# Centring three experts' first-layer weights on chip instead of their products, in a perceiver layer with KAN experts

## The chip, the cores and the metric
One core of one Trainium2 chip runs the whole kernel. The metric is the device time of one execution in microseconds; lower is better. The matrix engine is TensorE (PE in the profile), the elementwise engines are VectorE (DVE), ScalarE (ACT) and GpSimd (POOL), and SyncE (SP) starts transfers. Each has its own in-order queue of instructions; they wait for each other with semaphores.

## What is computed
A block of three parts over x (4 x 128 tokens, 128 features): cross attention on 2048 keys, a small attention over the four batch entries, and a mixture of experts. Only the last part is touched:

```python
logits = x @ gate_W                                # 8 experts, top 2 of them per token
h = gelu(einsum(x, mlp_W1) + mlp_b1);  mlp_out = einsum(h, mlp_W2) + mlp_b2      # experts 0..3
h0 = layernorm(x) * g0 + b0                                                       # experts 4..7 (KAN)
basis0 = 1 - tanh((h0[..., None] - grid) * 0.5) ** 2          # 8 grid points per feature
z = basis0.reshape(E2, T, 128 * 8) @ kan_sl_W0 + kan_sl_b0    # first KAN layer, 256 outputs
h1 = (z - z.mean(-1)) / sqrt(z.var(-1) + 1e-5) * g1 + b1      # layernorm over the 256 outputs
basis1 = 1 - tanh((h1[..., None] - grid) * 0.5) ** 2
kan_out = basis1 @ kan_sl_W1 + kan_sl_b1                      # second KAN layer
out = sum over the token's two experts of weight * expert_out
```

All is float32. The mean of z over its 256 outputs is linear in the weights: centring each row of `kan_sl_W0` over the 256 outputs (and the bias too) makes a z whose mean is zero.

## The kernel before
The kernel is one program with one block for each engine; the order in every queue is written by hand. It has an attention stage (to about 58 us in the profile), a short routing stage (to 70 us), and `ffn`, the experts. Tokens chosen for an expert are gathered into 160 slots by matmuls with one-hot matrices. In SBUF `kw0` holds the first KAN layer's weights, [128 features, 4 experts, 8 grid points, 256 outputs], loaded by one transfer at the start.

Each engine's part in the first KAN layer, for expert n = 0..3:

- VectorE: `choose(n)` (L1511, L1509) writes the one-hot columns, `keep_tokens(n)` (L1517 and L1520) keeps the gathered tokens, `squares0(n)` (L1529) squares the tanh values in two halves. `keep_z(n)` (L1535 to L1538) brings z from PSUM to SBUF (`zs`, as minus the product plus a constant). `centre(n)` subtracts the mean (L1542, into `zd`) and squares (L1545, into `zq`).
- ScalarE: `basis0(n)` (L699) computes eight tanh pieces of expert n. `residuals` (L687) makes four tiles for the very end.
- TensorE: `gather(n)` (L1015), `layer0(n)` (L1027): two halves of 128 outputs, c = 0 and 1, each over 8 grid points; `means(n)` (L1036): the mean of z over partitions and both halves by a matrix filled with 1/256; `variances(n)` (L1042): the same for the squares, one output row per expert. After the last of them `up` and `down` (L1062, L1072) are the first four experts, `spread` brings the inverse deviations back to all partitions, `layer1` (L1083) is the second KAN layer.

TensorE issues in `ffn`:

```python
gather(0); gather(1)
for n in range(E2):
    layer0(n)                  # from n = 2: variances(n - 2) between its two halves
    if n: means(n - 1)
    gather(n + 2)
means(3); variances(2); gather(6); variances(3); up(0); gather(7); up(1); ...
```

VectorE issues, from the point where z of expert 0 is there: keep_z(n), centre(n - 1) if n, keep_tokens(n + 2), squares0(n + 2) if n < 2, choose(n + 4) if n < 3 (and choose(7) at n = 2).

In the attention stage VectorE keeps scores (`keep_scores`, L1218), subtracts the maximum (`shift`, L1225 and L1228), takes sums (`keep_sums`, L1233), divides (`divided`, L1336 and L1338), forms the projected rows (`centred`, L1343) and their products (`products`, L1348). GpSimd has little to do in it: `mbias` (L520), `xb` (L524), and one root at 62 us (`rstd1`, L527). `keep_awake` (L928) is a set of matmuls whose results nobody reads.

## Time and profile before

| what | value |
|---|---|
| three runs, us | 149.10 median, 147.71 to 150.28 |
| the profiled execution, us | 146.81 |
| its span, first to last instruction, us | 144.6 |
| TensorE busy in the span | 133.3 us, 92% |
| VectorE / ScalarE / GpSimd busy | 72% / 50% / 31% |
| mean granted TensorE clock | 0.978 of 2.4 GHz |

The busy time of an engine is not its work at full rate: TensorE's matmuls are pipelined and their ends are modelled. The profile also gives the chain of work that ended last, tables of busy time for any stretch, and each engine's instructions in order of time with the idle time before them and its releaser.

### The profile page before, as it was taken

How to read it: one execution, taken by the hardware profiler on the slowest of the kernel's cores; microseconds unless marked ns; L12 is line 12 of the kernel's file. 1: busy time of each engine (PE TensorE's matmuls, PEld its weight loads, DVE VectorE, ACT ScalarE, POOL GpSimd, SP SyncE). 2: the span in 40 equal slices, each digit the busy share in tenths (PEclk: the TensorE clock that was granted, in tenths of full speed). 3: DMA queues.
4: the chain of work that ended last, by engine and by line, in shares of the span. 5: the costliest groups of instructions: out<-in, count | busy, mean ns of one | idle time of the engine just before them, and what ended most of it. 6: DMA issues, size and time to landing. Idle time of an engine off the chain costs nothing.

```text
span 144.6 us, 2952 instructions
## 1 busy us (share of the span) xinstructions
PE 133.3 (92%) x1070; PEld 102.7 (71%) x1070; DVE 104.2 (72%) x343; ACT 71.6 (50%) x175; POOL 45.1 (31%) x57
## 2 busy tenths in 40 slices
PE   6699999899999999899699999999999896899991
PEld 2255755455564666689489997988889895899980
DVE  0449979995798772579899696968445899983123
ACT  1258766665686776218290256200554996730110
POOL 8629000000000000026000377639300499787000
PEclk9999999999999999978999999999999999999995
DMA  4599999940000000599300000000000000001242
GB/s 134 149 323 461 435 415 372 389 141 0 0 2 5 7 0 0 145 430 435 156 0 5 0 2 1 2 10 0 2 0 0 18 11 18 23 27 43 33 133 77
DMA packets 6549, 15.93 MB, mean 110 GB/s; under 512 B 1456, under 2 KB 5008, under 8 KB 6016
## 3 DMA queue, kind: packets, MB, share of 16 engines
q1 hardware_dynamic: 5168, 14.73, 26.6%
q0 software_dynamic: 640, 0.51, 1.3%
q10 hardware_dynamic: 720, 0.43, 1.3%
q8 instruction: 11, 0.18, 0.5%
q14 instruction: 10, 0.08, 0.2%
HBM read 14.37 MB, written 1.38 MB: 109 GB/s over the span
## 4 chain that ended last, share of the span: by engine, by line
PE 46%; DVE 24%; POOL 10%; DMA 7%; issue 6%; ACT 2%; POOLq 1%; SPq 1%; DVEq 0%; ACTq 0%
POOL y_table L552 10%; PE C L819 9%; PE D L806 6%; DVE arena L1218 5%; PE A L1027 5%; PE A L796 5%; PE C L1015 4%; DMA arena<-ctxT 3%; PE A L1062 3%; DVE arena L1529 3%; DVE arena L1509 3%; DMA arena<-y_table 3%; PE D L1072 2%; PE A L1042 2%; DMA y_table<-arena,slot 1%
## 5 line engine op out<-in xcount | busy, mean ns | idle before, releaser
L625 ACT ACTIVATE arena<-C 128x512 f32<-128x512 f32 x32 | 18.9, 594 | 12.1 <-PE C L819 11.6
L1218 DVE CUSTOM_DVE_ANT_0 arena<-A,arena 128x512 f32<-128x512 f32 x32 | 20.2, 686 | 4.3 <-PE A L796 4.3
L552 POOL DMA_INDIRECT y_table<-arena,slot x12 | 16.9, 1408 | 14.7 <-DVE arena L1600 11.3
L819 PE MATMUL C<-cst,arena 128*128 128x128 f32 x128 | 20.5, 284 | 0.5 <-ACT arena L625 0.3
L819 PEld LDWEIGHTS C<-cst,arena 128*128 128x128 f32 x128 | 13.6, 141 | 9.3 <-issue 6.8
L1027 PE MATMUL A<-arena,kw 128*128 128x161 f32 x128 | 18.8, 301 | 0.3 <-DVE arena L1529 0.3
L1083 PE MATMUL D<-arena 128*128 128x161 f32 x128 | 18.6, 301 | 0.4 <-DVE arena L1580 0.4
L1027 PEld LDWEIGHTS A<-arena,kw 128*128 128x128 f32 x128 | 17.7, 189 | 1.1 <-issue 0.6
L1083 PEld LDWEIGHTS D<-arena 128*128 128x128 f32 x128 | 17.7, 189 | 0.9 <-issue 0.7
L527 POOL TENSOR_TENSOR rstd<-var,mhalf 128x4 f32<-128x4 f32 x1 | 1.0, 1025 | 47.6 <-DVE var L1380 47.6
L542 POOL DMA_INDIRECT slot_table<-pair,dest x8 | 9.1, 1136 | 15.3 <-DVE pair L1485 13.2
L806 PE MATMUL D<-arena 128*32 128x128 f32 x256 | 13.4, 284 | 0.0
L1580 DVE TENSOR_TENSOR arena<-arena 128x320 f32<-128x320 f32 x32 | 13.2, 479 | 0.0
L699 ACT ACTIVATE arena<-arena 128x160 f32<-128x160 f32 x32 | 7.7, 322 | 11.2 <-DVE arena L1517 11.2
L719 ACT ACTIVATE arena<-arena 128x320 f32<-128x320 f32 x32 | 11.7, 467 | 0.0
L1015 PE MATMUL C<-arena,xf 128*128 128x160 f32 x64 | 10.3, 303 | 1.2 <-DVE arena L1509 1.2
L616 ACT ACTIVATE arena<-arena,nmxb 128x512 f32<-128x512 f32 x16 | 11.4, 716 | 0.0
L1015 PEld LDWEIGHTS C<-arena,xf 128*128 128x128 f32 x64 | 9.0, 189 | 2.1 <-issue 1.1
L796 PE MATMUL A<-arena 32*128 32x512 f32 x64 | 9.1, 640 | 1.0 <-DVE mx L1218 0.6
L806 PEld LDWEIGHTS D<-arena 128*32 128x32 f32 x256 | 5.1, 108 | 5.3 <-issue 2.8
L1529 DVE TENSOR_TENSOR arena<-arena 128x640 f32<-128x640 f32 x8 | 6.5, 824 | 2.3 <-ACT arena L699 2.2
L1228 DVE TENSOR_SCALAR arena<-arena,nmxb 128x512 f32<-128x512 f32 x16 | 7.4, 505 | 0.3
(209 smaller groups left out, 213.6 us busy)
## 6 DMA issues: line engine op xcount, KB each, us to landing
kw<-KW SPq DMA_DIRECT2D x1, 4096.0 KB, 16.4
arena<-KW SPq DMA_DIRECT2D x1, 4096.0 KB, 13.6
mw<-MW SPq DMA_DIRECT2D x2, 1024.0 KB, 19.8
arena<-ctxT SPq DMA_DIRECT2D x4, 256.0 KB, 7.8
arena<-mask SPq DMA_DIRECT2D x1, 768.0 KB, 9.6
y_table<-zeros SPq DMA_DIRECT2D x1, 512.0 KB, 21.3
arena<-y_table SPq DMA_DIRECT2D x2, 256.0 KB, 3.2
arena<-mask SPq DMA_DIRECT2D x1, 256.0 KB, 7.8
```

The source lines that it names most:

```text
L552: pool.indirect_dma_start(out=y_table, out_offset=bass.IndirectOffsetOnAxis(ap=slot[0:m, j, n, 0:1], axis=0), in_=yn[0:m, n, j], in_offset ...
L616: act.activation(S[:, b % SBUFS, h], S[:, b % SBUFS, h], ACT.Identity, bias=nmxb[:, b, h:h + 1], scale=1.0).then_inc(shifted_act, 1)
L625: act.activation(PT[:, m % 4], C[m % 2][:, :], ACT.Exp).then_inc(probsT_kept, 1)
L719: i = act.activation(T1[:, n % 2, g], zs[:, n], ACT.Tanh, bias=tanh_bias(g))
L796: last = mm(BANK[j], QM[32 * j:32 * j + 32, u, b], kT[32 * j:32 * j + 32, b], start=True, stop=True)
L806: last = mm(sums[VW * j:VW * (j + 1), g * P:(g + 1) * P], v[:, 4 * g + j], probsT[:, j * P:(j + 1) * P], start=False, stop=True, skip_grou ...
L819: last = nc.tensor.transpose(C[m % 2][:, j * P:(j + 1) * P], S[:, b % SBUFS, 4 * g + j, t * P:(t + 1) * P], ident)
L1015: last = mm(X[n % 2][:, 0:SLOTS], xf[:, i], onehot[:, n % 4, i], start=(i == 0), stop=(i == B - 1))
L1027: last = mm(Z[n % 2][:, c * (SLOTS + 1):(c + 1) * (SLOTS + 1)], kw0[:, n, g, c * P:(c + 1) * P], SQ0[:, n % 2, g], start=(g == 0), stop=(g ...
L1083: last = mm(Y[n % 2], kw1[:, n, c, g], SQ1[:, n % 2, g, c], start=(g == 0 and c == 0), stop=(g == G - 1 and c == 1))
L1218: last = v.tensor_tensor_reduce(S[:, b % SBUFS, h], BANK[j], mbias[:, b], 1.0, -NEG, ALU.add, ALU.max, mx0[:, b, h:h + 1])
L1580: ins = v.tensor_tensor(SQ1[:, n % 2, g:g + 2, c, 0:SLOTS], t, t, ALU.mult)
```

## The change
For experts 1, 2 and 3 the weights in `kw0` are centred over their 256 outputs before use. VectorE sums them (`sum_weights`, in pieces between its attention work) and scales the sum to minus the mean (`low_weights`); GpSimd adds it for expert 1, and ScalarE for experts 2 and 3 (`centre_weights`, between the tanh groups). The bias is centred once (`sb0`), with one small matmul for its sum over partitions. So `means(1..3)` and the subtractions of these experts go; `square(n)` squares `zs` directly. Expert 0 keeps its mean product. The order in `ffn` changes too: variances(0) and variances(1) both stand between the halves of layer0(2), variances(2) between those of layer0(3); square(1) and square(2) stand last in their passes on VectorE, and `residuals` comes after basis0(3). `kw0`'s transfer has a semaphore of its own. Without `zd` the arena is smaller.

```diff
-            sp.dma_start(kw0[:], KW0).then_inc(ffn_in, 16)
+            sp.dma_start(kw0[:], KW0).then_inc(kw0_in, 16)
...
+            pool.wait_ge(kw0_lowered, 1)
+            for g in range(G):
+                last = nc.gpsimd.tensor_scalar(kw0[:, 1, g], kw0[:, 1, g], kw0_low[:, 1, g:g + 1], None, ALU.add)
+            last.then_inc(kw0_centred_pool, 1)
...
+            def centre_weights(n):
+                act.wait_ge(kw0_lowered, n)
+                for g in range(G):
+                    ins = act.activation(kw0[:, n, g], kw0[:, n, g], ACT.Identity, bias=kw0_low[:, n, g:g + 1], scale=1.0)
+                ins.then_inc(kw0_centred_act, 1)
...
-                    if n == 2 and not again:
+                    if n in (1, 2) and not again:
+                        centre_weights(n + 1)
+                    if n == 3 and not again:
                         residuals()
...
+            mm(SB0_SUM, mean_w[:], vec[:, SB0:SB0 + 2 * E2], start=True, stop=True).then_inc(sb0_summed, 1)
             keep_awake(4)
...
                 def layer0(n):
                     if n >= 2:
                         pe.wait_ge(z_kept, r * E2 + n - 1)
+                    if n and not again:
+                        pe.wait_ge(*weights_centred(n))
                     for c in range(2):
-                        if c == 1 and n >= 2:
-                            variances(n - 2)
+                        if c == 1 and n == 2:
+                            variances(0)
+                            variances(1)
+                        if c == 1 and n == 3:
+                            variances(2)
...
                 for n in range(E2):
                     layer0(n)
-                    if n:
-                        means(n - 1)
+                    if n == 1:
+                        first_means()
                     gather(n + 2)
-                means(3)
-                variances(2)
                 gather(6)
                 variances(3)
...
+            def sum_weights(n, lo, hi):
+                own(v.tensor_reduce(kw0_sum[:, n, lo:hi], kw0[:, n, lo:hi], AX, ALU.add))
+
+            def low_weights(n):
+                own_done()
+                v.tensor_scalar(kw0_low[:, n], kw0_sum[:, n], -1.0 / F2, None, ALU.mult).then_inc(kw0_lowered, 1)
...
             shift(2, 0)
+            dve.wait_ge(kw0_in, 16)
+            sum_weights(1, 0, 4)
             keep_scores(2, 1)
             shift(2, 1)
             keep_sums(0)
+            sum_weights(1, 4, 6)
             keep_scores(3, 0)
...
+            sum_weights(1, 6, 8)
+            low_weights(1)
             keep_scores(3, 1)
             shift(3, 1)
...
+            sum_weights(2, 0, 4)
             centred(0)
             centred(1)
             products((0, 0), (0, 1), (1, 1))
             divided(2)
+            sum_weights(2, 4, 8)
+            low_weights(2)
+            sum_weights(3, 0, 4)
             centred(2)
             keep_sums(3)
+            sum_weights(3, 4, 6)
             divided(3)
...
+            dve.wait_ge(sb0_summed, 1)
+            own(v.tensor_reduce(sb0_mean[:], SB0_SUM.rearrange("p (n c) -> p n c", c=2), AX, ALU.add))
+            own_done()
+            own(v.tensor_tensor(sb0[:], ..., ALU.subtract))
             dve.wait_ge(rstd1_made, 1)
...
+                def square(n):
+                    if n == 0:
+                        dve.wait_ge(mean_made, r + 1)
+                        v.tensor_tensor(zs[:, 0], zs[:, 0], MEAN[:, 0:SLOTS]..., ALU.subtract).then_inc(zd_made, 1)
+                        dve.wait_ge(zd_made, r + 1)
+                    else:
+                        dve.wait_ge(z_kept, r * E2 + n + 1)
+                    v.tensor_tensor(zq[:, n], zs[:, n], zs[:, n], ALU.mult).then_inc(zq_made, 1)
...
                 for n in range(E2):
                     keep_z(n)
-                    if n:
-                        centre(n - 1)
+                    if n == 1:
+                        square(0)
+                    if n == 3:
+                        square(3)
                     keep_tokens(n + 2)
+                    if n == 0 and not again:
+                        own(v.tensor_reduce(kw0_sum[:, 3, 6:8], kw0[:, 3, 6:8], AX, ALU.add))
+                        own_done()
+                        v.tensor_scalar(kw0_low[:, 3], kw0_sum[:, 3], -1.0 / F2, None, ALU.mult).then_inc(kw0_lowered, 1)
                     if n + 2 < E2:
                         squares0(n + 2)
                     if n < 3:
                         choose(n + 4)
                     if n == 2:
                         choose(7)
-                centre(3)
+                    if n in (1, 2):
+                        square(n)
                 keep_tokens(6)
```

## Rows read from the trace of the kernel before

**Rows 1.** Table of windows: stretch, length, then busy (instructions) by engine, clock.

```profile
core 0: us, PE busy (x) PEld busy (x) DVE busy (x) ACT busy (x) POOL busy (x), PEclk, DMA share, GB/s
29.40:58.20 28.80, 28.74 (x347) 17.22 (x348) 20.98 (x74) 19.95 (x36) 0.00 (x0) 1.00 0.05 15
...
87.90:102.50 14.60, 14.60 (x100) 12.58 (x100) 10.38 (x30) 3.20 (x9) 10.40 (x8) 1.00 0.03 3
```

**Rows 2.** The chain that ended last, 90 to 102 us: start, us, engine, line.

```profile
90.96 0.54 PE A L1036 x4
91.51 1.09 PE C L1015 x8
92.59 2.19 PE A L1027 x16
...
99.43 0.60 PE A L1036 x4
...
100.67 1.28 PE C L1015 x8
```

**Rows 3.** TensorE in order of time: start, us, line, out<-in, [idle before <-releaser].

```profile
85.36 2.35 PE L1027 MATMUL A<-arena,kw 128*128 128x161 f32 x16
87.87 0.71 PE L1042 MATMUL A<-arena,row_w 128*4 128x160 f32 x4 [0.16 <-DVE arena L1545]
88.51 2.45 PE L1027 MATMUL A<-arena,kw 128*128 128x161 f32 x16
```

**Rows 4.** VectorE in order of time, 87 to 96 us.

```profile
87.33 0.49 DVE L1545 TENSOR_TENSOR arena<-arena 128x320 f32<-128x320 f32 x1
...
89.25 1.73 DVE L1529 TENSOR_TENSOR arena<-arena 128x640 f32<-128x640 f32 x2 [1.08 <-ACT arena L699]
90.90 1.22 DVE L1511 TENSOR_SCALAR arena<-cst,posm,roots 128x160 f32<-128x160 f32 x4
92.05 0.14 DVE L1535 TENSOR_TENSOR arena<-A,vec 128x2 f32<-128x2 f32 x1
...
93.98 2.27 DVE L1511 TENSOR_SCALAR arena<-cst,posm,roots 128x160 f32<-128x160 f32 x8
```

**Rows 5.** Groups by line and shape: VectorE's reductions. Busy us, mean ns.

```profile
L1244 DVE TENSOR_REDUCE flags<-arena 128x4 f32<-128x1536 int32 x1 | 1.7, 1747 | 0.0
...
L1245 DVE TENSOR_REDUCE flags<-arena 128x4 f32<-128x512 int32 x1 | 0.7, 676 | 0.0
```

**Rows 6.** VectorE in order of time: idle time before three attention operations.

```profile
44.34 0.69 DVE L1218 CUSTOM_DVE_ANT_0 arena<-A,arena 128x512 f32<-128x512 f32 x1 [0.26 <-PE A L796]
...
53.29 0.61 DVE L1343 SCALAR_TENSOR_TENSOR cx<-A,notwipe,xba 128x129 f32<-128x129 f32 x2 [1.08 <-PE A L920]
...
57.58 0.35 DVE L1343 SCALAR_TENSOR_TENSOR cx<-A,notwipe,xba 128x129 f32<-128x129 f32 x1 [2.60 <-PE A L920]
```

**Rows 7.** Groups by shape and time rows: GpSimd and ScalarE prices, and VectorE beside GpSimd.

```profile
L616 ACT ACTIVATE arena<-arena,nmxb 128x512 f32<-128x512 f32 x16 | 11.4, 716 | 0.0
...
L547 POOL TENSOR_SCALAR arena<-token_row,slot 128x512 f32<-128x512 f32 x2 | 3.1, 1573 | 3.3 <-DMA slot<-slot_table 3.3
...
13.68 1.23 DVE L1228 TENSOR_SCALAR arena<-arena,nmxb 128x512 f32<-128x512 f32 x2
...
17.59 0.88 DVE L1228 TENSOR_SCALAR arena<-arena,nmxb 128x512 f32<-128x512 f32 x2
...
82.11 1.92 ACT L699 ACTIVATE arena<-arena 128x160 f32<-128x160 f32 x8 [6.06 <-DVE arena L1517]
...
88.21 1.92 ACT L699 ACTIVATE arena<-arena 128x160 f32<-128x160 f32 x8 [3.01 <-DVE arena L1517]
```

**Rows 8.** Windows around the clock's fall, keep_awake's durations (min/median/max), TensorE's longest wait.

```profile
62.00:63.00 1.00, 0.86 (x7) 0.67 (x7) 0.95 (x8) 0.28 (x1) 0.78 (x1) 1.00 1.21 524
...
65.00:66.00 1.00, 1.00 (x6) 1.00 (x6) 0.86 (x5) 0.73 (x3) 0.60 (x2) 0.50 0.94 393
...
L928 PE MATMUL D<-cst x36: 275/275/582, 58.9 to 67.3; 128*128 128x128 f32 x36
...
PE C L1093 <- DVE arena L1594: 1.7, 1, 1.7
```

More of the change, by code:

```diff
@@ L86, in layer @@
         kw0 = sb("kw0", [P, E2, G, F2])
+        kw0_sum = sb("kw0_sum", [P, E2, G])
+        kw0_low = sb("kw0_low", [P, E2, G])
+        sb0_mean = sb("sb0_mean", [P, E2])
+        sb0 = sb("sb0", [P, E2, 2])
         mw1 = sb("mw1", [P, E2, F])
@@ L163, in layer @@
         over_i = sb("over_i", [1, 1], I32)
-        ARENA = 31440
+        ARENA = 30900
         arena = sb("arena", [P, ARENA])
@@ L212, in layer @@
         zs = part(E2 * 2 * SLOTS, "p (n c s) -> p n c s", n=E2, c=2)
-        zd = part(E2 * 2 * SLOTS, "p (n c s) -> p n c s", n=E2, c=2)
         zq = part(E2 * 2 * SLOTS, "p (n c s) -> p n c s", n=E2, c=2)
@@ L251, in layer @@
         MEAN = A[1][:, 0:512]
+        SB0_SUM = C[1][:, 256:256 + 2 * E2]
         VAR = A[1][0:E2, 512:512 + SLOTS]
@@ L375, in layer @@
         mean_made = sem("mean_made")
+        kw0_in = sem("kw0_in")
+        kw0_summed = sem("kw0_summed")
+        kw0_lowered = sem("kw0_lowered")
+        kw0_centred_act = sem("kw0_centred_act")
+        kw0_centred_pool = sem("kw0_centred_pool")
+        sb0_summed = sem("sb0_summed")
         zd_made = sem("zd_made")
@@ L430, in load_word, with weights_centred @@
             return eng.value_load(word_i[0:1, 0:1])
+        def weights_centred(n):
+            return (kw0_centred_pool, 1) if n == 1 else (kw0_centred_act, n - 1)
         def rows_kept(r, n):
@@ L961, in _ @@
             project(B - 1)
-            pe.wait_ge(ffn_in, 64)
+            pe.wait_ge(ffn_in, 48)
+            pe.wait_ge(kw0_in, 16)
             pe.wait_ge(cxT_kept, 1)
@@ L1029, in layer0, with first_means @@
                     last.then_inc(z_made, 1)
-                def means(n):
-                    pe.wait_ge(z_kept, r * E2 + n + 1)
-                    if n:
-                        pe.wait_ge(zd_made, r * E2 + n)
+                def first_means():
+                    pe.wait_ge(z_kept, r * E2 + 1)
                     for c in range(2):
-                        last = mm(MEAN[:, 0:SLOTS], mean_w[:], zs[:, n, c], start=(c == 0), stop=(c == 1))
+                        last = mm(MEAN[:, 0:SLOTS], mean_w[:], zs[:, 0, c], start=(c == 0), stop=(c == 1))
                     last.then_inc(mean_made, 1)
@@ L1390, in by_column @@
                 return ap.unsqueeze(1).broadcast_to([P, B, B])
+            dve.wait_ge(sb0_summed, 1)
+            own(v.tensor_reduce(sb0_mean[:], SB0_SUM.rearrange("p (n c) -> p n c", c=2), AX, ALU.add))
+            own_done()
+            own(v.tensor_tensor(sb0[:], vec[:, SB0:SB0 + 2 * E2].rearrange("p (n c) -> p n c", c=2),
+                                sb0_mean[:].unsqueeze(2).broadcast_to([P, E2, 2]), ALU.subtract))
             dve.wait_ge(rstd1_made, 1)
@@ L1534, in keep_z @@
                     z = Z[n % 2][:, 0:2 * (SLOTS + 1)].rearrange("p (c s) -> p c s", c=2)
-                    step(v.tensor_tensor(cz[:, n], z[:, :, SLOTS], vec[:, SB0 + 2 * n:SB0 + 2 * n + 2], ALU.add))
+                    step(v.tensor_tensor(cz[:, n], z[:, :, SLOTS], sb0[:, n] if n else vec[:, SB0:SB0 + 2], ALU.add))
                     step_done()
@@ L1556, in scale @@
                     dve.wait_ge(spread_made, r * E2 + n + 1)
-                    v.tensor_tensor(zq[:, n], zd[:, n], X[n % 2][:, 0:SLOTS].unsqueeze(1).broadcast_to([P, 2, SLOTS]), ALU.mult
+                    v.tensor_tensor(zq[:, n], zs[:, n], X[n % 2][:, 0:SLOTS].unsqueeze(1).broadcast_to([P, 2, SLOTS]), ALU.mult
                                     ).then_inc(scaled, 1)
```

9 lines of the change are left out of this document (2 added, 7 removed).

## The prediction
> **What bounds the kernel now.** I read the table of windows first, stage by stage, to see which engine is full where [rows 1]. In the attention stage (29.4 to 58.2 us) TensorE is busy 28.74 of 28.80 us. In the stretch that the change aims at, 87.9 to 102.5 us (the second half of layer0(2) up to the last variance sum), it is busy 14.60 of 14.60 us while VectorE has 10.38. Then I read the chain that ended last over this stretch [rows 2]: it is a row of TensorE pieces with nothing between them, and that means that every matmul taken out here pays one for one, and every wait put into TensorE's queue costs one for one. Last I read TensorE's and VectorE's instructions in order of time, to see what each piece waits for [rows 3, 4]. The tail behind 102.5 us has two long strands, GpSimd's scatters one after another and TensorE's layer 1 and combine, and they end within half a us of each other. Both hang on the last variance sum, so a delay there moves all of it.
>
> **What is taken away.** Three of four `means` go (n = 1, 2, 3). The pieces cost 0.54 (twice) and 0.60 us in the chain; gather(6), whose 1.28 us hold a first matmul that doesn't overlap with one before, would take 1.09 behind another gather [rows 2]. Sum: 1.87 us off TensorE's row, all in the stretch where TensorE is full. On VectorE three subtractions of 0.48 us go as well, but VectorE is not the bound there.
>
> **What the new order of waits costs.** This is the main term. TensorE executes in order. In the middle of layer0(2), before its second half, it now issues variances(0) and variances(1). The second needs the squares of expert 1, `zq_made` 2. On VectorE `square(1)` no longer stands beside `keep_z(1)`: in the pass n = 1 it comes last, behind keep_tokens(3), squares0(3) and choose(5). VectorE is in order too. Its own rows show when these ran [rows 4]: squares0(3) from 89.25 (held 1.08 us by ScalarE's tanh for expert 3, which itself started at 88.21 when keep_tokens(3) was done [rows 7]), choose(5) from 90.90, and the next instruction at 92.05. So square(1) starts at about 92.1, takes 0.49 us like the square at 87.33 [rows 4], and TensorE may go on at 92.6. TensorE arrives there at 88.51: first half of layer0(2) from 85.36 for 2.35, variances(0) at 87.87, the second half at 88.51 [rows 3]. **Wait: 92.6 - 88.5 = 4.1 us.**
>
> Next I carried both queues on with durations from the same rows. variances(1) 0.64 (87.87 to 88.51), second half of layer0(2) 2.4: z of expert 2 is ready at 95.65. gather(4) 1.09 until 96.7, first half of layer0(3) 2.19 until 98.9 [rows 2, 3]. There variances(2) wants square(2). VectorE: keep_z(2) 95.7 to 96.5, keep_tokens(4) behind gather(4) at 96.8 for 0.25, then choose(6) and choose(7), 2.27 us for eight one-hot pieces [rows 4], and only then square(2), 99.3 to 99.8. **Second wait: about 0.9 us.** Then variances(2) 0.64, layer0(3)'s second half 2.38, gather(5) and gather(6) 1.09 each, variances(3) 0.64: done at 105.65, where it was 102.55. Behind variances(3) stands `up(0)` and behind it everything else; nothing there has slack for 3 us. Net: 4.1 + 0.9 - 1.9 = **+3.1 us**. Bounds of this term: the second wait could be 0.4 (if the one-hot pieces run closer) or 1.4, so 2.6 to 3.6.
>
> **The clock.** A wait of 4.1 us is longer than any idle time that TensorE had in the stages before the end: the longest is 1.7 us, shortly before 123.4 us, and the page shows no lower clock behind it [rows 8]. But after the thin stretch before 63 us (seven instructions in the last us, where attention has 347 in 28.8) it fell to 0.50, that is from 2.4 to 1.2 GHz, and came back about 3.4 us later, within the us from 66 to 67; a 128-column matmul there takes up to 582 ns where 275 is usual [rows 8]. So I expect the clock to fall in the new wait and the matmuls after it to run at half speed for a while. Bounds: nothing, if it stays; 3.4 us at half speed, as in that stretch, lose 1.7 us of work; two such stretches 3.4 us. These matmuls (second half of layer0(2), gather(4)) are on the path. I take **+1.5 us**.
> The Trainium skill says the same in "TensorE: Matmul & The Clock Gate" (Part 1: an idle array is throttled to half rate and activity releases it); by that rule the loss is certain in kind, and taken as certain it would make the sum 0.2 us larger.
>
> **The weights' centring.** Sums over 256 features of 8 grids for 3 experts are 6144 elements per partition on VectorE. Reductions of 1536 and 512 elements took 1.75 and 0.68 us [rows 5], so 1.05 ns for one more element: 1024 elements 1.21 us, 512 elements 0.68 us. The first two pieces of expert 1 (1024 and 512 elements) go where VectorE waits for the next scores, with idle time enough: free. The third, 512 elements and `low_weights(1)`, 0.85 us with the small scalar operation, comes before keep_scores(3,1), where VectorE has 0.26 us [rows 6]: these scores are kept 0.6 us later. TensorE's to_queries(0) needs them more than 1 us after they were kept, so that covers it. For expert 2, 1024 elements come before centred(0) (idle 1.08: about 0.1 over), then 1024, a small one and 1024, 2.65 us, before centred(2) (idle 2.60 [rows 6]). TensorE's transposes wanted centred(2) 0.14 us after it was done, so some 0.1 us shows. The 512 before divided(3) fit into its wait for TensorE.
> GpSimd adds expert 1's mean in 8 operations of 128x256. Its 128x512 with a per-partition operand took 1573 ns [rows 7], so up to 0.79 us each and 6.3 together: from 45 until 51.3 at most, long before its next work (rstd1, at 62.2) and layer0(1) (79.3). But it runs beside VectorE: when GpSimd was adding `xb`, the pair of VectorE's 128x512 `shift` operations took 1.23 us instead of 0.88 [rows 7]. So shift(3,1), the `xba` subtraction and the first sum of expert 2 may each be 0.3 us longer, and divided(2), whose result TensorE wants at 55.05, comes that much late. For the attention stage I take **+0.3 us**, from 0 (all inside the gaps) to 1.0 (each overlap in full).
> ScalarE adds the means of experts 2 and 3: 8 operations of 128x256 each. Its 128x512 with a per-partition bias took 716 ns, its 128x160 0.24 us start to start (eight in 1.92 [rows 7]); that gives 0.3 to 0.5 us each, 2.5 to 4 us for eight. The first eight lie in an idle time of 6.06 us before basis0(2), free. The second eight start at 84.0 and may last until 88.0; basis0(3) starts at 88.21 [rows 7]: free, with as little as 0.2 us to spare. If that cover were gone, basis0(3), squares0(3), square(1) and so TensorE's wait would all be later by the overhang.
> The Trainium skill ("ScalarE: Activation LUTs", What ACT_TABLE_LOAD costs) gives about 280 ns + 0.83 ns per column with a 93 ns overlap, an estimate of 0.40 us each and 3.2 us for eight: by it the second eight end at 87.2 and stay covered.
> The last sum of expert 3 (0.68 + 0.2 us) goes into VectorE's 1.08 us wait before squares0(2): free. The `residuals` moved behind basis0(3) end at 91.4 and are wanted at the very end: free. The centred bias `sb0` (a small matmul, two small VectorE operations, 0.2 us each beside the other small ones) lies in the 0.36 us in which VectorE waits for rstd1: **+0.1 us**, from 0 to 0.3. The smaller arena moves addresses only, the split semaphore of the `kw0` load costs nothing: the load lands near 25 us, its first reader comes at 33.
>
> **Sum.** 3.1 + 1.5 + 0.3 + 0.1 = +5.0 us. The profiled execution took 146.81 us with a span of 144.6; its span would be 149.6. The median of the three runs is 149.1 (147.71 to 150.28), 2.3 above the profiled one, and the difference is carried over: **154.1 us**.
>
> **Rivals.**
> - The clock does not fall, or its loss falls into VectorE's time: +3.5, 152.6 us. For it: no fall after the idle 1.7 us [rows 8]. Against it: the new wait is more than twice that.
> - The centring is not hidden: GpSimd holds VectorE up in full, ScalarE's eight take 0.5 us each, and the clock stays low twice as long: 3.1 + 3.4 + 1.0 + 0.3 = +7.8, 156.9 us.
> - Not slower: VectorE reaches both squares in time. Then only the 1.87 us count and the time is 147.3 us with the small costs. It decides at the sum of the two waits: under 1.9 us the change gains. For it: TensorE is full there, so anything removed is gained. Against it: square(1) would have to be done by 90.4, before choose(5) even starts, and no instruction in VectorE's row between 89.25 and 92.05 is removed by the change.
> - The waits are half as long as worked out, and the clock holds: +0.5 to +2, about 150.5 us.
>
> **How the numbers follow.** Forecast 0.66, clock holds 0.16, centring not hidden 0.07, not slower 0.06, half waits 0.05. About 2% (3 us) is what a measurement of this kernel can tell from no change, 146.1 to 152.1. Slower by more: the forecast, the dear case and 0.11 of the second case, 0.84. Within: 0.14 (the rest of the second case, the half waits and 0.04 of the case not slower). Faster by more: 0.02, since even the whole saving is 1.3%. The range runs from 151.2 (first term at its lower bound and the clock kept, 151.7, less half a us for the scatter of the runs) to the dear case, 156.9; below it lie the cases not slower and half waits, 0.11 together, and above it a little.
>
> **What would show it.** Right: TensorE idle for about 4 us before the L1042-type matmuls in the middle of layer0(2), released by the VectorE square; a second, shorter one before variances(2); a granted clock of 0.5 within them or behind; ScalarE's second eight ending before basis0(3) starts; TensorE's row up to the first gather at most 0.5 us later. Wrong: TensorE unbroken from 88 to 100 us, or the loss sitting before 70 us.

## The result and the profile after

| | before | after |
|---|---|---|
| median of the executions timed in turn, us | 148.52 (4; 147.71 to 150.28) | 154.94 (4; 154.71 to 156.97) |
| ratio after / before | | 1.053 [1.044, 1.063] |
| profiled execution / its span, us | 146.81 / 144.6 | 155.05 / 153.2 |

The change makes the kernel 5.3% slower, some 6.5 to 9.3 us by the interval. Some executions of a kernel are slow ones, 1.5% or more longer than its fastest, so ratios here and below compare fast executions alone and are not the quotients of the medians. The two profiled executions lie 8.2 us apart (spans: 8.6), which is the upper part of the interval: the profiled execution of before, at 146.81 us, was shorter than all four that were timed. Everything below accounts for the 8.6 us between the two traces.

First the page of the changed kernel. Each digit of its row of granted clock is a slice of 3.83 us. The clock dips twice in the middle of the experts, in the slices from 92 to 99.6 us and in the one from 103.4 to 107.3. No slice around 65 us is low, where before had its dip. That dip comes in some executions only and costs nothing at that place, since the first gather behind it is released by VectorE: wait_filled_2, a run below, has it (0.50 from 64 to 66 us) and needs 27.54 us from VectorE's sum of `wo` to the first gather, as the changed kernel does without it.

```profile
span 153.2 us, 2963 instructions
...
PEclk9999999999999999999999997895999999999998
```

Then its table of windows (stretch, length, then busy time and instructions of PE, PEld, DVE, ACT and POOL, granted clock, DMA share, GB/s). The first row answers to the attention row of [rows 1]: TensorE has the same 28.8 us of work in a stretch that is 0.8 us longer, VectorE is at 27.7 us where it had 21.0, and GpSimd has its eight additions. The second, from the middle of layer0(2) to variances(3), shows what is new: TensorE has 16.2 us of work in 22.5.

```profile
29.40:59.00 29.60, 28.77 (x347) 17.20 (x348) 27.66 (x81) 19.95 (x36) 7.95 (x8) 1.00 0.03 10
...
88.70:111.20 22.50, 16.18 (x89) 13.85 (x89) 10.63 (x27) 4.37 (x13) 10.80 (x8) 0.85 0.02 2
```

TensorE in order of time over that stretch (start, us, line, out<-in, count, [idle before <-releaser]). It answers to [rows 3]. L1074 is `variances`, L1061 `layer0`, L1044 `gather`.

```profile
88.71 0.71 PE L1074 MATMUL A<-arena,row_w 128*4 128x160 f32 x4 [0.18 <-DVE arena L1600]
93.42 0.85 PE L1074 MATMUL A<-arena,row_w 128*4 128x160 f32 x4 [4.00 <-DVE arena L1600]
94.20 3.94 PE L1061 MATMUL A<-arena,kw 128*128 128x161 f32 x16
97.98 1.25 PE L1044 MATMUL C<-arena,xf 128*128 128x160 f32 x8
99.06 2.35 PE L1061 MATMUL A<-arena,kw 128*128 128x161 f32 x16
103.72 0.91 PE L1074 MATMUL A<-arena,row_w 128*4 128x160 f32 x4 [2.31 <-DVE arena L1600]
104.56 3.88 PE L1061 MATMUL A<-arena,kw 128*128 128x161 f32 x16
108.28 2.33 PE L1044 MATMUL C<-arena,xf 128*128 128x160 f32 x16
110.54 0.71 PE L1074 MATMUL A<-arena,row_w 128*4 128x160 f32 x4
```

Two idle times, 4.00 and 2.31 us, both ended by VectorE's square (L1600), and behind each one a half layer that takes 3.9 us where the one between them takes 2.35. The windows inside the second and third half layer give the clock there:

```profile
94.20:98.00 3.80, 3.80 (x18) 3.80 (x18) 0.00 (x0) 0.00 (x0) 0.45 (x1) 0.60 0.05 6
...
104.50:108.30 3.80, 3.80 (x18) 3.74 (x18) 0.00 (x0) 0.00 (x0) 0.00 (x0) 0.61 0.02 4
```

VectorE in the same stretch, to be read beside [rows 4]. The first three rows are squares0(3), choose(5) and square(1), the last two choose(6) with choose(7), and square(2).

```profile
90.09 1.73 DVE L1581 TENSOR_TENSOR arena<-arena 128x640 f32<-128x640 f32 x2 [1.08 <-ACT arena L724]
91.74 1.23 DVE L1563 TENSOR_SCALAR arena<-cst,posm,roots 128x160 f32<-128x160 f32 x4
92.89 0.48 DVE L1600 TENSOR_TENSOR arena<-arena 128x320 f32<-128x320 f32 x1
...
99.50 3.76 DVE L1563 TENSOR_SCALAR arena<-cst,posm,roots 128x160 f32<-128x160 f32 x8
103.19 0.48 DVE L1600 TENSOR_TENSOR arena<-arena 128x320 f32<-128x320 f32 x1
```

The same eight one-hot pieces took 2.27 us in [rows 4]; now they take 3.76. GpSimd's row in time says what runs beside them: its four comparisons for the slot table (L566; two over 128 partitions, two over 32), 1.56 us each, from 97.55 to 103.77.

```profile
97.55 6.22 POOL L566 TENSOR_SCALAR arena<-token_row,slot 128x512 f32<-128x512 f32 x4 [3.35 <-DMA slot<-slot_table]
```

In before these comparisons ran from 96.36 to 102.59 and the one-hot pieces from 93.98 to 96.25: just in front of them.

**The account of the 8.6 us.** The first gather starts at 70.84 where it was 70.02: +0.82. From the start of variances(0) to that of variances(3) it is 21.83 us (88.71 to 110.54) where it was 14.01 (87.87 to 101.88): +7.82. The two together are 8.64, the last variance sum's own shift is 8.66, and the span's is 8.6: the tail moved as a block.

### The profile page after: what moved, and what is told of

Its sections match the earlier page's. It is cut to its first block, busy times and chain, and to the rows that moved or that the text cites. A ratio compares the mean times of both kernels' runs of the same rounds, so it can differ in the third digit from the quotient of the medians.

```text
span 153.2 us, 2963 instructions
## 1 busy us (share of the span) xinstructions
PE 133.9 (87%) x1060; PEld 102.7 (67%) x1060; DVE 112.7 (74%) x353; ACT 78.0 (51%) x191; POOL 53.2 (35%) x65
## 3 DMA queue, kind: packets, MB, share of 16 engines
HBM read 14.37 MB, written 1.38 MB: 103 GB/s over the span
## 4 chain that ended last, share of the span: by engine, by line
PE 47%; DVE 40%; issue 4%; DMA 3%; ACT 3%; SPq 1%; DVEq 0%; ACTq 0%
PE D L1115 8%; DVE arena L1248 6%; PE C L846 6%; PE A L1061 5%; PE A L823 4%; DVE arena L1563 4%; DVE arena L1635 4%; PE C L1044 4%; PE D L833 4%; DMA arena<-ctxT 3%; PE A L1094 3%; DVE arena L1581 3%; PE A L1163 3%; DVE arena L1561 2%; ACT arena L724 2%
## 5 line engine op out<-in xcount | busy, mean ns | idle before, releaser
L1061 PE MATMUL A<-arena,kw 128*128 128x161 f32 x128 | 21.7, 331 | 0.3 <-DVE arena L1581 0.3
L1061 PEld LDWEIGHTS A<-arena,kw 128*128 128x128 f32 x128 | 20.6, 215 | 1.4 <-issue 0.9
L542 POOL TENSOR_SCALAR kw<-kw,kw_low 128x256 f32<-128x256 f32 x8 | 8.0, 1009 | 30.9 <-DVE kw_low L1270 30.9
L1044 PE MATMUL C<-arena,xf 128*128 128x160 f32 x64 | 10.0, 302 | 1.8 <-DVE arena L1561 1.8
L1044 PEld LDWEIGHTS C<-arena,xf 128*128 128x128 f32 x64 | 9.0, 190 | 2.4 <-issue 1.3
L1074 PE MATMUL A<-arena,row_w 128*4 128x160 f32 x16 | 3.2, 324 | 6.5 <-DVE arena L1600 6.5
```

Of the source, the lines that this page charges most:

```text
L1044: last = mm(X[n % 2][:, 0:SLOTS], xf[:, i], onehot[:, n % 4, i], start=(i == 0), stop=(i == B - 1))
L1061: last = mm(Z[n % 2][:, c * (SLOTS + 1):(c + 1) * (SLOTS + 1)], kw0[:, n, g, c * P:(c + 1) * P], SQ0[:, n % 2, g], start=(g == 0), stop=(g ...
```

## The theory and its rivals

The theory was that of the prediction: square(1) and square(2) stand too late in VectorE's queue for the places of variances(1) and variances(2) in TensorE's, TensorE waits, and the clock falls behind the waits. What the trace alone can't tell:

- whether the place of the squares on VectorE makes the loss, or the place of the variances on TensorE, or both only together;
- whether the slow half layers come from the clock, and whether their loss is on the path;
- why the second wait is 2.31 us and not 0.9: GpSimd beside the one-hot pieces, or something else;
- where the 0.8 us ahead of the first gather come from.

All experiments are edits of the changed kernel.

## Experiments on the two waits

**squares_early: the squares right behind what they need.** In VectorE's pass n = 1 square(1) goes in front of squares0(3) and choose(5); square(2) goes in front of choose(6).

```diff
-                    if n == 3:
-                        square(3)
+                    if n >= 2:
+                        square(n)
                     keep_tokens(n + 2)
+                    if n == 1:
+                        square(1)
...
-                    if n in (1, 2):
-                        square(n)
```

> The changed kernel with one thing put back: on VectorE square(1) stands right behind keep_tokens(3) and square(2) right behind keep_z(2), instead of last in their passes. Theory A (TensorE waits in order for late squares, and the clock falls in these waits): both waits of the changed kernel (4.0 and 2.3 us) shrink to under 0.4 us, the granted clock stays 1.00 from 88 us on, and the last variance sum comes at about 101.5 us instead of 110.5; span 143.5 to 144.8 us, 8.5 to 9.5 under the changed kernel, ratio to the kernel before 0.99 to 1.00. Theory B (the centring work itself, its reductions and the shared memory port of GpSimd and VectorE, costs most of it): the time falls by 3 us at most, ratio 1.03 or more.

Measured: median 146.96 us (145.17 to 148.37), ratio to before 0.993 [0.975, 1.011], span 144.0. TensorE in order of time from the same point on:

```profile
88.85 1.46 PE L1074 MATMUL A<-arena,row_w 128*4 128x160 f32 x8 [0.18 <-DVE arena L1600]
90.24 2.46 PE L1061 MATMUL A<-arena,kw 128*128 128x161 f32 x16
...
101.10 0.71 PE L1074 MATMUL A<-arena,row_w 128*4 128x160 f32 x4
```

Both variance sums now run as one row of eight, no idle time stands before the half layer, and variances(3) starts at 101.10, 9.4 us earlier than in the changed kernel. From the first gather to variances(3) it is 30.11 us (70.99 to 101.10) for 39.70 in the changed kernel (70.84 to 110.54), so 9.59 less, which is the two waits and the clock of the account at the end (4.00 + 2.31 + 3.26) to 0.02 us. The one-hot pieces are back at 2.27 us and the clock is full. Moving two VectorE instructions gives back all that was lost there.

**old_places: the variances back in their old places, the squares left late.**

```diff
-                        if c == 1 and n == 2:
-                            variances(0)
-                            variances(1)
-                        if c == 1 and n == 3:
-                            variances(2)
+                        if c == 1 and n >= 2:
+                            variances(n - 2)
...
+                variances(2)
                 gather(6)
                 variances(3)
```

> The changed kernel with the variance products put back where the kernel before has them (one between the halves of layer0(2), one in layer0(3), variances(2) after gather(5)); the squares stay last in VectorE's passes. Theory A: what costs is the pair (late square, early wait), so undoing TensorE's side alone cures as much as undoing VectorE's side: no wait over 0.5 us on TensorE between 88 and 102 us, ratio 0.985 to 1.005, within 0.7 us of the version with the squares early. Theory C (the late squares push VectorE's other work, the gathers' one-hot columns and kept tokens, and these delay TensorE by themselves): 2 us or more of TensorE waits remain before gathers, ratio over 1.01.

Measured: median 146.0 us (145.3 to 146.73), ratio 0.997 [0.986, 1.007], span 144.0.

```profile
88.75 0.71 PE L1071 MATMUL A<-arena,row_w 128*4 128x160 f32 x4
...
95.05 0.71 PE L1071 MATMUL A<-arena,row_w 128*4 128x160 f32 x4
...
101.08 0.71 PE L1071 MATMUL A<-arena,row_w 128*4 128x160 f32 x4
```

There is no idle time in front of any of them. From the start of variances(0) to that of variances(3) it is 12.33 us, where squares_early has 12.25 (88.85 to 101.10) and the changed kernel 21.83. So neither the late squares nor the early variances cost more than 0.1 us alone: the loss needs the late producer and the early consumer together, in two queues that both run in order. That the two executions agree in span and in the start of variances(3) is chance: this one started 0.98 us earlier (sum of `wo` at 42.46 for 43.44) and lost 0.88 us between the first gather and variances(0), where its clock was at 0.50 from 72.4 to 75.9 us.

**slots_later: GpSimd's comparisons moved behind the one-hot pieces.** GpSimd waits for square(2) before its four comparisons, so they can't run beside choose(6) and choose(7). Everything else stays, both late squares too.

```diff
             pool.wait_ge(slots_in, 32)
+            pool.wait_ge(zq_made, 3)
             for e in range(SENT, EX):
```

> The changed kernel with one wait more on GpSimd: its own_slot comparisons (6.2 us) start only when the squares of expert 2 are made, so they no longer run beside choose(6) and choose(7). Theory D (the eight one-hot pieces took 3.76 instead of 2.27 us because GpSimd ran beside them): the pieces take 2.3 us, TensorE's second wait 0.8 to 1.0 instead of 2.3 us, and if the clock then doesn't fall a second time another 1.4 us is saved: span 1.4 to 2.9 us under the changed kernel. If GpSimd has nothing to do with it: pieces 3.7 us, span unchanged within 0.4 us.

Measured: median 153.84 us (153.18 to 154.31), ratio 1.050 [1.039, 1.060], span 151.3. VectorE's one-hot pieces:

```profile
99.84 2.27 DVE L1564 TENSOR_SCALAR arena<-cst,posm,roots 128x160 f32<-128x160 f32 x8
```

TensorE's second wait and the half layer behind it:

```profile
102.56 0.71 PE L1075 MATMUL A<-arena,row_w 128*4 128x160 f32 x4 [0.81 <-DVE arena L1601]
103.20 2.46 PE L1062 MATMUL A<-arena,kw 128*128 128x161 f32 x16
```

GpSimd's comparisons:

```profile
102.69 6.21 POOL L567 TENSOR_SCALAR arena<-token_row,slot 128x512 f32<-128x512 f32 x4 [8.16 <-DVE arena L1601]
```

With GpSimd out of the way the pieces take 2.27 us again and the second wait is 0.81 us, the 0.9 of the prediction. And the half layer behind it runs at full speed, 2.46 us: the second fall of the clock was a consequence of the longer wait. From the first gather to variances(3) it is 36.57 us (71.19 to 107.76) where the changed kernel has 39.70: 3.13 less, of which 1.50 are idle time, 1.42 the half layer and 0.20 variances(2). The span gains only 1.9 us: the first gather was 0.35 us later in this execution, and the tail behind variances(3) takes 43.5 us for 42.7, with GpSimd's comparisons ending at 108.9 instead of 103.8. That they are what makes the tail longer wasn't tried; in the profiled executions of the other edited kernels the tail took 42.1 to 43.2 us, so part of it may be scatter.

The shape of the collision shows when the changed kernel's rows are read one instruction at a time:

```profile
99.12 1.58 POOL L566 TENSOR_SCALAR arena<-token_row,slot 32x512 f32<-32x512 f32 x1
...
99.89 0.35 DVE L1563 TENSOR_SCALAR arena<-cst,posm,roots 128x160 f32<-128x160 f32 x1
...
100.16 0.68 DVE L1563 TENSOR_SCALAR arena<-cst,posm,roots 128x160 f32<-128x160 f32 x1
```

All eight one-hot pieces run beside a comparison. Three of them take 0.35 us, as they do alone (0.36 in slots_later), the first takes 0.46, and four take 0.68 to 0.74. So the 1.49 us are lost in steps of 0.33 to 0.39 by four of the pieces (and 0.1 by the first), and no piece was held up for a whole comparison. GpSimd can lose as well: in wait_filled_2, another run below, its first two comparisons took 1.87 and 1.93 us for 1.56. The Trainium skill ("SBUF — State Buffer", SBUF: two separate sides) says of the port pair that VectorE and GpSimd share that the pair is locked for a whole instruction and the other engine blocked until then. These rows don't agree with it as it stands: the piece from 99.89 to 100.24 started and ended within the comparison from 99.12 to 100.69, at its usual length. What decides which piece is slowed isn't shown.

## Experiments on the clock

**wait_filled: matmuls that nobody reads in both waits.** The edit puts 34 matmuls of 128 columns in front of variances(1) and 17 in front of variances(2), so that TensorE doesn't stand idle there.

```diff
                         if c == 1 and n == 2:
                             variances(0)
+                            if not again:
+                                for _ in range(34):
+                                    mm(BANK[2][:, 0:P], ident, ident, start=True, stop=True, skip_group_check=True)
                             variances(1)
                         if c == 1 and n == 3:
+                            if not again:
+                                for _ in range(17):
+                                    mm(BANK[2][:, 0:P], ident, ident, start=True, stop=True, skip_group_check=True)
                             variances(2)
```

> The changed kernel with idle-time matmuls (128x128, 0.11 us each, results unread) in TensorE's two waits: 34 between variances(0) and variances(1), 17 before variances(2). The waits' ends are set by VectorE as before. If the clock is a cost of its own: granted clock 1.00 from 88 to 112 us, the half of layer0(2) behind the wait takes 2.4 us instead of 3.9, the same for layer0(3), and the span is 2.5 to 3.0 us under the changed kernel, ratio 1.03 to 1.04. If the low clock only falls into time in which VectorE would have been waited for anyway: under 1 us.

Measured: median 158.32 us (156.66 to 160.82), ratio 1.072 [1.051, 1.094], span 154.8. The fillers were sized wrongly:

```profile
88.69 7.86 PE L1057 MATMUL A<-cst 128*128 128x128 f32 x68
```

34 matmuls of float32 are 68 instructions of 0.115 us in the trace and took 7.86 us, twice the wait. The rows of the half layers, x16 for eight matmuls, had shown the same doubling. Still, the half layers behind the fillers took 2.45 and 2.46 us. The next kernel has half as many.

**wait_filled_2: 17 and 10 of them.**

```diff
-                                for _ in range(34):
+                                for _ in range(17):
...
-                                for _ in range(17):
+                                for _ in range(10):
```

> The filled waits again, now with the right size: in the first try 34 matmuls took 7.9 us, twice what was meant, because a float32 matmul is two instructions of 0.115 us. Now 17 (3.9 us) between variances(0) and variances(1), and 10 (2.3 us) before variances(2). If the clock's loss is on the path by itself: clock 1.00 throughout, both halves behind the waits 2.3 us long, last variance sum at 107.5 to 108 us instead of 110.5, span 150.2 to 150.8, ratio 1.02 to 1.04. If not, the span stays at 153.

Measured: median 153.3 us (150.99 to 154.32), ratio 1.043 [1.034, 1.053], span 149.2.

```profile
89.27 4.06 PE L1057 MATMUL A<-cst 128*128 128x128 f32 x34
93.98 2.45 PE L1067 MATMUL A<-arena,kw 128*128 128x161 f32 x16
...
99.55 2.39 PE L1062 MATMUL A<-cst 128*128 128x128 f32 x20
102.51 2.45 PE L1067 MATMUL A<-arena,kw 128*128 128x161 f32 x16
107.07 0.71 PE L1080 MATMUL A<-arena,row_w 128*4 128x160 f32 x4
```

The fillers take 4.06 and 2.39 us, about as long as the waits were. Both half layers take 2.45 us, and variances(3) starts at 107.07 instead of 110.54, 3.47 us earlier. Not all of that is the clock: 0.07 us are an earlier variances(0), and 0.15 us come from a shorter stretch between gather(4) and variances(2), where the second wait had changed its cause. GpSimd's comparisons started later in this execution (98.93), the one-hot pieces took 3.09 us, square(2) was done at 101.3, and it was the fillers that held variances(2) until 101.87. What is left, 1.63 us behind the first fillers and 1.62 behind the second, together 3.25 us, is the clock's price on the path. The changed kernel's own rows give the same against before: 3.78 - 2.29 (start to start of the half layer behind the first wait) = 1.49, two variance sums 0.14 and 0.20 longer, and 3.72 - 2.29 = 1.43 for the second, together 3.26 us. So the idle times themselves are 4.00 + 2.31 us and the half speed behind them about 3.3. The span came out 1.0 us under the expected range, as variances(3) is 0.4 us before its own range and the tail took 42.1 us for 42.7.

The rows say which idle times in the experts were followed by half speed: 4.00 us and 2.2 to 2.3 us in every run that left them empty, 0.81 us in front of variances(2) not. That doesn't clear short waits everywhere: in old_places the clock fell at 72.4 us, behind two waits of 0.97 and 0.81 us at the first two gathers, which other executions pass at full clock. By the Trainium skill ("TensorE: Matmul & The Clock Gate", Part 1) an idle array is throttled to half rate and work releases it; that agrees. The price isn't fixed. In four executions with the empty first wait the half layer behind it took 3.94, 4.05, 4.66 and 4.66 us (the last two in no_gpsimd and no_third_sum, below). Their clocks differ in when they fell, which a window of half a us shows, first for the changed kernel and then for no_gpsimd:

```profile
93.50:94.00 0.50, 0.50 (x4) 0.18 (x3) 0.00 (x0) 0.00 (x0) 0.50 (x1) 0.84 0.00 0
...
91.50:92.00 0.50, 0.00 (x0) 0.00 (x0) 0.50 (x3) 0.50 (x1) 0.43 (x1) 0.84 0.00 0
```

In the changed kernel the clock fell at 93.8 us, just after TensorE had begun to work again, and was low until 97.3; in slots_later likewise, from 94.3 to 97.7. In no_gpsimd it fell at 91.8, inside the wait, and was low until 98.7. From variances(1) to the first half of layer0(3) the changed kernel takes 5.64 us and no_gpsimd 6.88 (slots_later 5.65, no_third_sum 6.76, wait_filled_2 4.01): against the last of these, one fall costs 1.6 us in two executions and 2.8 to 2.9 in the other two.

## Experiments on the 0.8 us ahead of the first gather

In the changed kernel the only new idle time of TensorE in the attention stage is in front of `numerator` (L943), which waits for divided(2):

```profile
55.89 0.33 PE L943 MATMUL A<-cst,arena 128*128 128x128 f32 x1 [0.76 <-DVE arena L1380]
```

On VectorE, the rows ahead of it. The pair at L1258, at 47.80, is shift(3,1); L1400 and L1405 are the `xba` subtraction and a small scalar one, L1266 the sum of 1024 elements of expert 2, L1385 centred(0) and centred(1). GpSimd's eight additions (L542) last until 52.94.

```profile
44.99 7.95 POOL L542 TENSOR_SCALAR kw<-kw,kw_low 128x256 f32<-128x256 f32 x8 [30.91 <-DVE kw_low L1270]
...
47.80 1.20 DVE L1258 TENSOR_SCALAR arena<-arena,nmxb 128x512 f32<-128x512 f32 x2
51.19 0.69 DVE L1400 TENSOR_TENSOR xba<-xb,xba 128x512 f32<-128x512 f32 x1
52.60 0.36 DVE L1405 TENSOR_SCALAR hvec<-vec 128x8 f32<-128x8 f32 x1
53.02 1.22 DVE L1266 TENSOR_REDUCE kw_sum<-kw 128x4 f32<-128x1024 f32 x1
54.16 0.60 DVE L1385 SCALAR_TENSOR_TENSOR cx<-A,notwipe,xba 128x129 f32<-128x129 f32 x2
```

**no_gpsimd: GpSimd's additions left out.** The mean of expert 1's weights is not subtracted (the sums and scalings stay); expert 1 is computed from weights that aren't centred. One profiled execution, without a ratio.

```diff
             for g in range(G):
-                last = nc.gpsimd.tensor_scalar(kw0[:, 1, g], kw0[:, 1, g], kw0_low[:, 1, g:g + 1], None, ALU.add)
-            last.then_inc(kw0_centred_pool, 1)
+                pass
+            pool.sem_inc(kw0_centred_pool, 1)
```

> The changed kernel without GpSimd's eight additions (expert 1's weights stay uncentred, the part that is left out). Shared-port theory: VectorE's shift before divided(0) takes 0.88 instead of 1.20 us, the small hvec operations 0.15 instead of 0.3, centred(0) starts 0.3 to 0.4 us earlier, and the first gather at 70.4 to 70.5 instead of 70.84. If GpSimd does not hold VectorE up: no change, 70.8.

**no_third_sum: the sum of 1024 elements before centred(0) left out.** Half of expert 2's row sums are zero, so half its weights aren't centred.

```diff
             own(v.memset(nmxh[:], NEG))
+            own(v.memset(kw0_sum[:, 2, 0:4], 0.0))
...
-            sum_weights(2, 0, 4)
             centred(0)
             centred(1)
```

> The changed kernel without the sum over four grids of expert 2 before centred(0) (left out; its means are wrong). If that sum is what makes divided(2) late: centred(0) starts when its projection is there, at 53.3, divided(2) at 54.5, and the first gather at 70.0 to 70.1, so the whole 0.8 us is gone although GpSimd still runs beside VectorE. If the earlier sum and GpSimd matter by themselves, 0.3 us or more remains.

Measured, the row at L943 in the first and the rows of centred(0) and at L943 in the second:

```profile
55.07 0.33 PE L943 MATMUL A<-cst,arena 128*128 128x128 f32 x1 [0.42 <-DVE arena L1380]
```

```profile
53.16 0.61 DVE L1386 SCALAR_TENSOR_TENSOR cx<-A,notwipe,xba 128x129 f32<-128x129 f32 x2 [0.30 <-PE A L947]
...
54.93 0.33 PE L943 MATMUL A<-cst,arena 128*128 128x128 f32 x1
```

Executions start some tenths of a us apart, so the distance is taken from one early VectorE operation, the sum of `wo` (at 43.30 in both before and after), to the first gather: before 26.73 us, after 27.54, no_gpsimd 27.31, no_third_sum 26.72. In the five other executions with the changed kernel's attention stage (squares_early, old_places, slots_later and both with filled waits) it is 27.54 or 27.55, so a difference of 0.2 us in a single execution is well clear of the scatter. Without GpSimd the wait shrinks by 0.34 us and the distance by 0.23. Without the sum the wait is gone, and with it all of the 0.8 us, though GpSimd ran beside VectorE as before (the shift pair took 1.20 us there too). So the sum is what carries the delay over to centred(0). It can be taken apart at centred(0), again from the sum of `wo`: 10.00 us in before (43.29 to 53.29 [rows 6]), 10.86 in the changed kernel (43.30 to 54.16), 10.52 in no_gpsimd (42.81 to 53.33). GpSimd's share is thus 0.34 us (the shift pair alone lost 0.32). The other 0.52 us: in before VectorE was free 8.92 us after that point (53.29 less 1.08 of waiting), and in no_gpsimd the sum starts at 9.38 (52.19), 0.46 late, since expert 1's last piece stands in front; and the sum fills 1.14 us of a gap of 1.08. The two executions took 155.0 and 155.6 us in total, with spans of 153.2 and 153.8, not less than the changed kernel: in both the half layer behind the first wait took 4.66 us, which eats what was gained in front of it. For that reason the distance and not the total is used.

**gaps_only: squares early, and the sums cut to VectorE's gaps.** The version that the experiments point to. All work of the change stays; of expert 1's sum five grids and then three go in front of keep_scores(2,1) and keep_scores(3,0), of expert 2's two, three and three grids into three gaps.

```diff
-            sum_weights(1, 0, 4)
+            sum_weights(1, 0, 5)
...
-            sum_weights(1, 4, 6)
+            sum_weights(1, 5, 8)
+            low_weights(1)
...
-            sum_weights(1, 6, 8)
-            low_weights(1)
+            sum_weights(2, 0, 2)
             keep_scores(3, 1)
...
-            sum_weights(2, 0, 4)
+            sum_weights(2, 2, 5)
             centred(0)
...
             divided(2)
-            sum_weights(2, 4, 8)
+            sum_weights(2, 5, 8)
```

(and the edit of squares_early)

> The version with the squares early, and the sums of the weights cut to the size of VectorE's gaps: 5 + 3 grids of expert 1 before keep_scores(3,0) (so GpSimd's additions end before divided(0)), 2 + 3 grids of expert 2 before keep_scores(3,1) and centred(0), its last 3 behind divided(2). If the attention stage's 0.8 us come from late sums (VectorE late for divided(2)), the first gather starts at 70.0 to 70.2 us as in the kernel before, and the span is 143.0 to 143.6, 0.8 under the squares early; ratio to the kernel before 0.98 to 1.00. If they come from something else (the longer kernel, another alignment), the first gather stays at 70.8.

Measured: median 144.89 us of 6 (144.2 to 147.11) against 148.5 of 11 for before, ratio 0.984 [0.977, 0.992], span 142.3.

```profile
54.68 0.33 PE L943 MATMUL A<-cst,arena 128*128 128x128 f32 x1 [0.33 <-DVE arena L1380]
69.64 1.32 PE L1044 MATMUL C<-arena,xf 128*128 128x160 f32 x8 [0.97 <-DVE arena L1561]
87.51 1.46 PE L1074 MATMUL A<-arena,row_w 128*4 128x160 f32 x8 [0.18 <-DVE arena L1600]
...
99.75 0.71 PE L1074 MATMUL A<-arena,row_w 128*4 128x160 f32 x4
```

The distance from the sum of `wo` to the first gather is 26.59 us, as short as before's. From the first gather to variances(3) it is 30.11 us (69.64 to 99.75; squares_early also 30.11), where before has 31.86 (70.02 to 101.88): 1.75 us less, which is the value of the three mean products when nothing waits. The rest of the 2.13 us by which variances(3) is earlier are 0.14 from the distance in front and 0.24 from an earlier start (the sum of `wo` at 43.05), which is also why the first gather and the span lie under the expected ranges. The change's idea is worth 1.6% of the time (0.8 to 2.3% by the interval); against that version, its order of instructions costs 7%.

## Why the prediction was right, and where it was off

The forecast, slower, 154.1 us within 151.2 to 156.9, holds: 154.94. By its steps, in the profiled executions:

| term | forecast | measured | shown by |
|---|---|---|---|
| mean products removed | -1.87 | -1.75 | gaps_only, squares_early |
| first wait | +4.1 | +4.00 | trace, squares_early |
| second wait | +0.9 (0.4 to 1.4) | +2.31 | trace; slots_later 0.81 |
| clock | +1.5 (0 to 3.4) | +3.26 | trace; wait_filled_2 3.25 |
| attention stage | +0.3 (0 to 1.0) | +0.82 | no_third_sum, no_gpsimd |
| `sb0` | +0.1 | 0 | rstd1 to its reader 1.13 us in both |
| sum | +5.0 | +8.64 | span +8.6 |

- **First wait.** Right in place, releaser and size. VectorE's order was carried on by hand from [rows 4] and each instruction ran where it was put, 0.8 us later as a whole, like TensorE.
- **Second wait, the term that was mis-sized.** The step said that choose(6) and choose(7) take 2.27 us as in [rows 4], and bounded the wait by 0.4 and 1.4. They took 3.76, outside the bound. The step took a duration from a stretch of before where GpSimd stood still, and put it into a stretch where, after the first wait had moved VectorE by 5.5 us, GpSimd's comparisons run. These are released by a transfer and not by TensorE, so the first wait didn't move them: 97.55 for 96.36. The prediction had the very price in hand, shift beside `xb` in [rows 7], but used it for the attention stage alone. slots_later shows 0.81 without the collision.
- **The clock.** Right that it falls, behind the first wait and for the reason given. One stretch costs 1.49 us and 0.14 for variances(1), as forecast; there were two. At a second wait of 0.81 us the clock stays (slots_later), so the second stretch follows from the error of the step before. The bound of two stretches, 3.4 us, held it in this execution. It is not a bound for every one: in no_gpsimd, whose clock fell inside the first wait, the two falls cost 2.87 and 1.67 us.
- **The attention stage.** Right that it is VectorE held up, with divided(2) late for TensorE; the amount is near the upper bound. The step that failed is that the sum before centred(0) is "about 0.1 over": it set the sum's 1.21 us (measured 1.22) against the whole gap of 1.08 us, as if VectorE came to it on time. It came 0.46 us late from the third piece of expert 1, which had been costed as covered by to_queries(0), and 0.34 us late from GpSimd. A gap can be filled once: a delay that has no reader of its own still takes from the next gap. no_third_sum and no_gpsimd show both parts.
- **GpSimd beside VectorE.** GpSimd's eight additions took 7.95 us and not at most 6.3; they were still in time. Read one by one, five took 0.92 to 0.94 us, and the three beside shift(3,1) and beside VectorE's copies and small operations after 51.8 us took 1.00, 1.08 and 1.38. So more than half of the miss is the estimate of 0.79 for one, and some 0.7 us go with what VectorE did beside them. The shift pair took 1.20 us for 0.88, as forecast. But the `xba` subtraction took 0.69 us as in before, though GpSimd ran beside it, and the first sum of expert 2 started at 53.02, when GpSimd had just ended. The Trainium skill ("SBUF — State Buffer", Who interferes with whom) has VectorE operations with two tensors from SBUF contend with a GpSimd operation that reads SBUF; this row doesn't show it for VectorE. The GpSimd addition that began within it, at 51.56, is the one that took 1.38, but other VectorE operations ran beside that one too. The same section has reductions never contend on this chip; that agrees: the `xb` sum took 0.67 us beside GpSimd and 0.68 without.
- **ScalarE.** Covered, as forecast: its second eight took 3.29 us (3.2 by the estimate), and basis0(3) started 0.99 us behind their end, released by keep_tokens(3), as ScalarE's rows of the changed kernel show at the end of this section.
- **The offset.** The total came out 0.8 us from the forecast although the trace's sum is 3.6 us above it. The prediction carried over 2.3 us from the profiled execution to the median of three; after's profiled execution was at its own median (155.05 and 154.94), so this added 2.3 us that weren't there (another 0.4 us is that the time exceeds the span by 2.2 us in before and by 1.9 in after). Part of the nearness is therefore luck: two errors of opposite sign.

```profile
84.77 3.29 ACT L705 ACTIVATE kw<-kw,kw_low 128x256 f32<-128x256 f32 x8
89.05 1.92 ACT L724 ACTIVATE arena<-arena 128x160 f32<-128x160 f32 x8 [0.99 <-DVE arena L1569]
```

**What stays open.** Why the clock falls inside the first wait in some executions and only behind it in others. What makes GpSimd's comparison slow one one-hot piece and leave the next alone.

## What to carry to other kernels

An instruction that waits in an in-order queue costs what its producer's own queue makes of it: when a consumer is moved forward or a producer back, write down both queues to the instruction and subtract, since either move alone was free here (to 0.1 us) and the two together cost 6.3 us of idle time and 3.3 of clock. Work that is taken out of a full engine is only gained if the new order has no wait: 1.75 us here, less than half of the first one. And when a wait shifts one engine against another, look up again what each shifted instruction now runs beside; its duration from the old trace is only good for its old neighbours.

## What the runs showed of the hardware

- TensorE's clock fell behind idle times of 4.00 and 2.3 us in the middle of full work and stayed down for about one half layer (3.8 to 4.7 us for 2.3 to 2.45). It did not behind a single 0.81 us there; in one execution (old_places) it fell behind two waits of 0.97 and 0.81 us at the first gathers. Filling the idle times with matmuls that nobody reads kept it at 2.4 GHz and gave back 3.25 us, though the waits stayed.
- When the clock fell inside the 4 us wait (91.8 us in no_gpsimd) it was low for 6.8 us and the fall cost 2.9 us; when it fell just behind the wait (93.8 us in the changed kernel) it was low for 3.4 us and cost 1.6.
- Eight VectorE tensor-scalar pieces of 128x160 took 3.76 us beside GpSimd's comparisons over 512 elements and 2.27 without them: four took 0.68 to 0.74 us each, the others 0.35 to 0.46, and none waited for a comparison (1.56 us) to end. Beside GpSimd's 128x256 additions a pair of 128x512 took 1.20 for 0.88, while a reduction over 512 elements (0.67) and a subtraction of two tensors (0.69) were not slowed.
- One float32 matmul is two instructions in the trace, of 0.115 us each at 128 columns.
